# Layer 0 sum pass: TensorE works on pairs of half tiles, and SyncE and GpSimd share the stacking of the keys

## What is computed

```python
q = (query @ Wq + bq).reshape(B, Nq, H, D).transpose(0, 2, 1, 3)      # 16 heads of width 16
k = (key_value @ Wk + bk).reshape(B, Nkv, H, D).transpose(0, 2, 1, 3) # 12544 keys
v = (key_value @ Wv + bv).reshape(B, Nkv, H, D).transpose(0, 2, 1, 3)
attn = softmax(clip(einsum('bhqd,bhkd->bhqk', q, k) * scale, -CLAMP, CLAMP))
x = einsum('bhqk,bhkd->bqhd', attn, v).reshape(B, Nq, Cq) @ Wo + bo
```

## Time and profile before

| | us |
|---|---|
| median of 3 runs (lowest, highest) | 1162.57 (1161.85, 1162.88) |
| the profiled execution | 1163.62 |
| its span in the trace | 1161.8 |
| sum pass of layer 0 in it | 264.2 to 644.5 |
| one chunk of it, undisturbed | 26.6 |
| everything after it | 517.3 |

### The profile page before, as it was taken

The page is one execution under the profiler, slowest core; times in us unless marked ns, Lnnn a source line. Parts: engine busy times, 40 slices in busy tenths (PEclk is TensorE's granted clock), DMA queues, the critical chain, the costliest instruction groups (busy, mean ns, idle before and its releaser), DMA issues.

```text
span 1161.8 us, 21208 instructions
## 1 busy us (share of the span) xinstructions
PE 958.8 (83%) x7648; PEld 702.1 (60%) x7651; DVE 645.5 (56%) x936; ACT 539.8 (46%) x626; POOL 176.2 (15%) x93
## 2 busy tenths in 40 slices
PE   3877888749899999999969578886999979998514
PEld 2544555537677777777747365555777767776403
DVE  4777999862111222222250237994779757777592
ACT  2787888626666666666646313002333323332011
POOL 4000000141111111111193031242004030000000
PEclk9978999878999999999999689998999989999665
DMA  7213121154556555566614332211001000000000
GB/s 209 82 30 120 48 70 57 33 126 95 129 128 152 131 126 126 134 146 145 144 32 97 109 101 56 64 36 32 1 5 33 1 6 1 1 1 1 1 0 5
DMA packets 37319, 81.73 MB, mean 70 GB/s; under 512 B 9553, under 2 KB 17426, under 8 KB 37138
## 3 DMA queue, kind: packets, MB, share of 16 engines
q1 hardware_dynamic: 37266, 81.01, 28.1%
HBM read 41.54 MB, written 0.13 MB: 36 GB/s over the span
## 4 chain that ended last, share of the span: by engine, by line
PE 46%; issue 19%; DVE 11%; SPq 9%; DMA 7%; ACT 6%; POOL 1%; DVEq 1%; ACTq 0%; POOLq 0%
PE ps L1498 10%; SPq L310 8%; DMA ks<-khl 6%; PE ps L1508 6%; PE ps L1291 5%; PE ps L1519 5%; PE ps L1303 4%; PE ps L1273 4%; PE ps L1245 4%; PE ps L1500 2%; DVE cm L813 2%; ACT pr L555 1%; DVE pr L819 1%; DMA raw<-in_ctxT 1%; PE ps L1282 1%
## 5 line engine op out<-in xcount | busy, mean ns | idle before, releaser
L617 ACT ACTIVATE pr<-ps 128x1024 f32<-128x1024 f32 x196 | 200.0, 1026 | 131.7 <-DVEq L966 127.9
L1291 PE MATMUL ps<-qs,ks 128*128 128x256 f32 x784 | 147.0, 310 | 21.8 <-DMA ks<-khl 13.9
L1245 PE MATMUL ps<-ks 128*128 128x448 f32 x448 | 134.5, 422 | 33.7 <-ACT pr L555 14.3
L1291 PEld LDWEIGHTS ps<-qs,ks 128*128 128x128 f32 x784 | 106.8, 192 | 64.2 <-issue 33.0
L695 ACT ACTIVATE pr<-ps 128x1024 f32<-128x1024 f32 x56 | 57.5, 1027 | 184.7 <-DVE ps L1096 184.7
L1498 PE MATMUL ps<-ks,ct 128*128 128x512 f32 x448 | 128.3, 408 | 7.2 <-issue 4.6
L813 DVE TENSOR_REDUCE cm<-ps 128x1 f32<-128x896 f32 x112 | 120.5, 1084 | 16.9 <-PE ps L1245 16.0
L1245 PEld LDWEIGHTS ps<-ks 128*128 128x128 f32 x448 | 80.7, 206 | 76.8 <-DVE cm L813 28.0
L1303 PE MATMUL ps<-pr,v 128*17 128x128 f32 x3136 | 124.6, 277 | 0.2 <-ACT pr L617 0.2
L847 DVE SCALAR_TENSOR_TENSOR khl<-ps,bk,khl 128x448 fp32r<-128x448 f32 x56 | 38.2, 682 | 151.0 <-ACT khl L592 151.0
L1096 DVE TENSOR_SCALAR ps<-ps 128x1024 f32<-128x1024 f32 x56 | 68.9, 1231 | 76.5 <-PE ps L1500 76.5
(11 more groups left out here) (259 smaller groups left out, 1325.6 us busy)
## 6 DMA issues: line engine op xcount, KB each, us to landing
ks<-khl SPq DMA_DIRECT2D x168, 224.0 KB, 4.8
raw<-in_ctxT SPq DMA_DIRECT2D x36, 448.0 KB, 3.7
raw<-in_ctxT SPq DMA_DIRECT2D x54, 224.0 KB, 4.2
ffw<-in_mask_q SPq DMA_DIRECT2D x1, 1568.0 KB, 10.0
ffw<-in_W1T SPq DMA_DIRECT2D x1, 1024.0 KB, 4.9
ffw<-in_W2T SPq DMA_DIRECT2D x1, 1024.0 KB, 7.2
pr<-in_Wq SPq DMA_DIRECT2D x1, 1024.0 KB, 5.1
pr<-in_Wkt SPq DMA_DIRECT2D x1, 1024.0 KB, 7.4
```

The lines of the kernel that those rows point to most:

```text
L617: nc.scalar.activation(pr[:, (HALVES * b + u) % 4, :], bank(2 * (u % 2), 2), ACT.Exp).then_inc(S["e0_exp"], 1)
L1245: last = mm(ps[:, bank + n, 0:NB], qn[:, h, :], kn[:, b, t, n * NB:(n + 1) * NB], start=True, stop=True)
L1291: last = mm(ps[:, 2 * z + k // 2, (k % 2) * 256:(k % 2) * 256 + 256], ks_v[:, b, gg, t * P:(t + 1) * P], qs[:, gg * 256:gg * 256 + 256], s ...
```

## The change

TensorE now handles half tiles in pairs (`chunk0` and `projections0`): two scores, then up to two key blocks or two value tiles of the next chunk, then two weighings. The value tiles alternate between banks 7 and 5. The tables of key and value positions are per pair. SyncE issues only the eight high transfers, and waits for ScalarE's last high block (`e0_khi`) in place of VectorE's low one; GpSimd's own queue issues the four low transfers (`stack_low_keys`), behind a one-element addition, ahead of `split_lo0` of the chunk after. ScalarE's copy of the raw context comes in two parts, after half tiles 7 and 9, and GpSimd's remainder waits for the second as before.

```diff
-KEYS_AT = [0, 1, 2, 3]
-VALUES_AT = [4, 5, 6, 7, 8, 9, 10]
+KEYS_AT = [[0, 1], [2, 3], [], [], [], [], []]
+VALUES_AT = [[], [], [0, 1], [2, 3], [4, 5], [6], []]
...
             def stack_keys(c, b):
-                sp.wait_ge(S["e0_klo"], 4 * c + 6)
+                sp.wait_ge(S["e0_khi"], 4 * c + 4)
...
-                for slot, part in ((0, 0), (1, 0), (2, 1)):
+                for slot in range(2):
...
+            def stack_low_keys(c, b):
+                pool.wait_ge(S["e0_klo"], 4 * c + 6)
+                pool.wait_ge(S["e0_score"], HALVES * (c + 1))
+                nc.gpsimd.tensor_tensor(pause[:, 2:3], pause[:, 1:2], pause[:, 1:2], ALU.add
+                                        ).then_inc(S["e0_low_go"], 1)
+                for g in range(4):
+                    pool.dma_start(ks_v[64:96, b, g::4, :].bitcast(F32),
+                                   khl[32 * g:32 * g + 32, 1, :, :].bitcast(F32)
+                                   ).then_inc(S[f"e0_low_keys{b}"], 16)
+                pool.wait_ge(S["e0_low_go"], c + 1)
...
-                    if keys and u - 1 in KEYS_AT:
-                        i = KEYS_AT.index(u - 1)
-                        key_block_hi(c + 1, i, 22 + 11 * (c + 1) + K_ORDER[i], (f"e0_keys{b}", 192 * (i2 + 1)))
-                    if split and u == 9:
-                        split_hi0(c + 2, b)
+                    if keys and 2 <= u < 6:
+                        i = u - 2
+                        key_block_hi(c + 1, i, 22 + 11 * (c + 1) + K_ORDER[i], (b, i2 + 1))
+                    if split and u in (7, 9):
+                        split_hi0(c + 2, b, halves=[(u - 7) // 2])
...
-                    if nxt:
-                        if u - 1 in KEYS_AT:
-                            key_block_lo(c + 1, KEYS_AT.index(u - 1))
-                        if u in VALUES_AT:
-                            t = VALUES_AT.index(u)
+                    if nxt and u % 2 == 1 and u > 1:
+                        for i in KEYS_AT[(u - 3) // 2]:
+                            key_block_lo(c + 1, i)
+                        for t in VALUES_AT[(u - 3) // 2]:
                             value_tile(c + 1, 1 - b, t, 22 + 11 * (c + 1) + V_ORDER[t])
...
+            def chunk0(c, b, i2, nxt):
+                for v in range(TPC):
+                    if v < TPC - 1:
+                        scores0(c, b, 2 * v + 2)
+                        scores0(c, b, 2 * v + 3)
+                    elif nxt:
+                        pe.wait_ge(S["ks_ones"], 2)
+                        pe.wait_ge(S[f"e0_keys{1 - b}"], 128 * (i2 + 1 + b))
+                        pe.wait_ge(S[f"e0_low_keys{1 - b}"], 64 * (i2 + 1 + b))
+                        scores0(c + 1, 1 - b, 0)
+                        scores0(c + 1, 1 - b, 1)
+                    if nxt:
+                        projections0(c + 1, 1 - b, v)
+                    weigh0(c, b, 2 * v)
+                    weigh0(c, b, 2 * v + 1)
```

More of the change, by code:

```diff
@@ L64, with value_bank @@
 PAIRS = [(W_AH, X_AH), (W_AL, X_AH), (W_AH, X_AL), (W_BH, X_B), (W_BL, X_B)]
-KEYS_AT = [0, 1, 2, 3]
-VALUES_AT = [4, 5, 6, 7, 8, 9, 10]
-K_ORDER = [1 + sorted(KEYS_AT + VALUES_AT).index(u) for u in KEYS_AT]
-V_ORDER = [1 + sorted(KEYS_AT + VALUES_AT).index(u) for u in VALUES_AT]
+KEYS_AT = [[0, 1], [2, 3], [], [], [], [], []]
+VALUES_AT = [[], [], [0, 1], [2, 3], [4, 5], [6], []]
+K_ORDER = [1, 2, 3, 4]
+V_ORDER = [5, 6, 7, 8, 9, 10, 11]
+def value_bank(t):
+    return 7 if t % 2 == 0 else 5
 TURNS = ["x0", "o0", "x1", "x2", "x3", "x4", "o4", "x5"]
@@ L414, in _ @@
             pool.wait_ge(S["e0_lo"], 3)
+            stack_low_keys(0, 0)
             pool.wait_ge(S["m0_ml"], 1)
@@ L418, in _ @@
             pool.wait_ge(S["ks_ones"], 2)
-            with pool.Fori(2, NCH, 2) as c:
+            with pool.Fori(0, NCH - 2, 2) as c:
                 for b in range(2):
-                    split_lo0(c + b, b)
+                    stack_low_keys(c + b + 1, 1 - b)
+                    split_lo0(c + b + 2, b)
+            stack_low_keys(NCH - 1, 1)
             pool.wait_ge(S["thr"], 1)
@@ L531, in key_block_max0, with split_hi0 @@
                                      bias=bk0[:, t:t + 1]).then_inc(S["m0_keys"], 1)
[L533 to L537, removed]
+            def split_hi0(c, b, halves=(0, 1)):
+                if 0 in halves:
+                    act.wait_ge(S["e0_raw"], 48 * (c + 1))
+                    act.wait_ge(S["e0_proj"], 11 * c + 11)
+                    nc.scalar.copy(ct[:, b, X_AH, :], raw[:, 0, :])
+                if 1 in halves:
+                    nc.scalar.copy(ct[:, b, X_B, :], raw[:, 1, :]).then_inc(S["e0_hi"], 1)
             def mask_sum(s):
@@ L1318, in _ @@
                     t = h - 8
-                    values0(0, 0, t, bank=7 if t % 2 == 0 else 4, emptied=1 if t == 0 else 0)
+                    pe.wait_ge(S["e0_v"], t + (1 if t == 0 else 0))
+                    values0(0, 0, t, 7 if t % 2 == 0 else 4)
             pe.wait_ge(S["m0_ml"], 1)
@@ L1341, in _ @@
             pe.wait_ge(S["ks_ones"], 1)
-            pe.wait_ge(S["e0_keys0"], 192)
+            pe.wait_ge(S["e0_keys0"], 128)
+            pe.wait_ge(S["e0_low_keys0"], 64)
             scores0(0, 0, 0)
[L1347 to L1364, removed]
-                step0(c, b, HALVES - 1, True, False)
-                step0(c + 1, 1 - b, 0, nxt, False)
-                weigh0(c, b, HALVES - 1)
+            def projections0(c, b, v):
+                for i in KEYS_AT[v]:
+                    if i == 0:
+                        pe.wait_ge(S["e0_v"], TPC * c)
+                    project0(c, b, i)
+                for t in VALUES_AT[v]:
+                    if t == 1:
+                        pe.wait_ge(S["e0_klo"], 4 * c + 5)
+                    pe.wait_ge(S["e0_v"], TPC * c + t + (1 if t == 0 else 0))
+                    values0(c, b, t, value_bank(t))
@@ L1369, in _ @@
             pe.wait_ge(S["nm"], 2)
-            step0(0, 0, 0, True, False)
+            scores0(0, 0, 1)
             pe.wait_ge(S["zero"], 1)
@@ L1376, in _ @@
                 for b in range(2):
-                    round0(2 * i2 + b, b, i2, True)
-            round0(NCH - 2, 0, NSUP - 1, False)
-            for u in range(1, HALVES):
-                step0(NCH - 1, 1, u, False, True)
-            weigh0(NCH - 1, 1, HALVES - 1)
+                    chunk0(2 * i2 + b, b, i2, True)
+            chunk0(NCH - 2, 0, NSUP - 1, True)
+            chunk0(NCH - 1, 1, NSUP - 1, False)
             pe.wait_ge(S["o0_read"], 1)
```

11 lines of the change are left out of this document (6 added, 5 removed).

## The result

| | before | changed |
|---|---|---|
| median, us (20 runs each) | 1162.37 | 1165.67 |
| lowest to highest | 1159.51 to 1164.24 | 1161.76 to 1168.78 |
| the profiled execution, its span | 1163.62, 1161.8 | 1168.78, 1167.0 |

The ratio is 1.003, with a 95% interval of 1.002 to 1.004: slower by 3.3 us between the medians. The forecast was 1116, so this is the place of rival 1. The profiled execution is the slowest of the 20, so the sums over its trace show a somewhat larger loss.

A forecast was written before the change was run, and what follows sets the result against it. TensorE and the stacking of keys were both taken as nearly at the limit in layer 0's sum pass. Savings of 47 us from 1163.6 gave 1116.5, about 1116 against the median; forecast range 1106 to 1127, wide range 1106 to 1166.

The forecast's parts named there:

- rival 1: Queues share DMA engines, S stays 15.1, TensorE idles 3.0 us a chunk, clock falls: 1172 us (1160 to 1177); chance 0.20.
- the pairs on TensorE: Layer 0's sum pass: a pair saves 0.3 us of switching; rounds 4.2 and 3.3 us, TensorE needs 23.4 a chunk.
- the sum: Savings added: chunk 0 -3.0, chunks 1 to 11 at 23.7 us each -33.7, chunk 12 -9.4, chunk 13 -1.0; together -47.
- the first transfer: First stacking transfer issued 11.2 us after the chunk's start, against 11.3 before: nothing gained.
- Chunk 12: 29.5 us for 38.87: 23.7, plus 4.3 for VectorE's table, plus 1.5 for unpackings; gain 9.4, bounds 4 and 11.
- Chunk 13: Bare chunk, 19.2 us before: six pairs save at most 2 us, taken as 1.
- S: Time from first stacking transfer's issue to last one's landing: 15.1 us before, forecast up to 12.5, bounds 10.7 and 15.1.
- The copy in two parts: ScalarE's split copy of the raw context fits the pauses between exponentials and costs nothing.
- the raw load: Next raw context load on SyncE, behind GpSimd's remainder, has a chunk's time to spare.
- the clock: In rival 1: TensorE's clock falls to 0.50 behind each long pause, priced at 1.6 us a chunk.
- Chunk 0: First chunk of the sum pass: forecast 27.9 to 24.9 us, -3.0; rival 1 put it at +1.
- Sign (b): While both queues run, DMA exceeds 300 GB/s; the last high transfer lands under 12.5 us after the first issue.

## Why the prediction was wrong

**Right: the pairs on TensorE.** Rounds of 4.2 and 3.3 us were forecast, 4.18 and 3.33 measured; 23.4 us a chunk, and 23.54 measured once nothing else was late. The switch saved per pair was taken as 0.3, and 1.92 / 7 is 0.27. The 23.7 of the sum is a slip of 0.1 (the mean of 23.4 and 11.2 + 12.5 is 23.6), worth 1 us.

**Right: the first transfer,** at 11.2, at full clock (11.1 with the filled pause). "Nothing is gained here" held.

**Chunk 12: the number near, in part by luck.** It took 28.18 us for 29.5. Right is that GpSimd's ternary work has moved behind the chunk's keys, 18.5 us of it into chunk 13, and that VectorE's unpackings then take their shortest, 0.28 to 0.29. But the table, said to stay at +4.3, did not stay: it went from 6.1 us (585.19 to 591.25) to 3.5 (600.51 to 603.97), with GpSimd's work gone from beside it, and the first exponential came 2.2 us after the scores instead of 5.2. And it is not TensorE that sets the 28.2 us but the stack, 12.6 to its first transfer and 15.5 for itself. With the stack out of the way the chunk takes 27.53. Chunk 13 gave 0.3 where 1 was taken; it begins behind a pause of 3.3 us, at a clock of 0.91 over the chunk.

**Wrong: the stack.** S was taken at 12.5 or less, "nearer to the lower end, since the row at 358 is stacking itself". It is 15.3, or 15.5 with the start of the scores. The step that failed takes the full overlap from a row of half a microsecond at a seam between two transfers. The row is real, and the changed kernel has such stretches (312 GB/s), but they don't last. As far as the orders tried tell, they come while the two queues have transfers of different halves of the partitions. Over a stack that is worth 0.4 to 0.8 us (the queues alone, 14.3 to 14.7 for 15.1), 1.7 in their last ordinary chunk, not 4.4. The rows at 209 and 358, both at a share over 1, could not say which pairs of transfers overlap; the bound of 15.1 was the honest end, and the value should have stayed near it. The rule of the Trainium skill (DMA: Bandwidth & Descriptors, "Issuing engines are not separate DMA queues"), which the prediction weighed and put at 0.20, agrees with the result to within these 0.8 us. In the section "Rules for kernel authors" of the same page the Trainium skill says of two transfers to disjoint halves of the partitions that they serialize. Here that is nearly so, and goes a little too far: at one busy share the order moved the rate between 227 and 246 GB/s on one queue and between 215 and 258 on two.

**Wrong: "The copy in two parts fits the pauses between exponentials: nothing", and the raw load has "a chunk's time to spare".** Being early was a harm. ScalarE's second copy ended 22.0 us after the chunk's start before, and ends 19.0 after it now (426.37 + 0.94 - 408.28); GpSimd's remainders end 3 us earlier with it, and the raw load, which they release, falls into the stack. Only about 0.9 of the 3 us is the first half of the copy, which no longer stands in front of the second; the rest comes with the pairs. By these figures, as an estimate, the load would go out a microsecond later without the copy in two parts, and still inside the stack. Price: 0.7 to 0.9 us a stack, and 1150 instead of 1165.7 where it is taken out. It has eaten what the second queue brought.

**Left out of the forecast, priced in rival 1: the clock.** A chunk was put at 23.7 and took 27.85 (306.4 / 11). Of the 4.15 between them, 3.0 are the stack (15.5 for 12.5) and 1.2 are TensorE's slow rounds ahead of the first transfer (12.36 for 11.2). Rival 1 had S = 15.1, a pause of 3.0 us (measured 2.6 to 3.1), a clock of 0.50 behind it (0.59 over 3.3 us), chunks 1 to 11 at 308 (measured 306.4). It put the end at 1172 and, if half the lost time hides, at 1164. Chunk 0 was worse than it said, +3.9 for +1: the clock is 0.71 up to its first transfer, which goes at 278.64, 14.6 us after the start (before, 0.80 and 12.2), and its stack takes 16.9 us (15.6 before). Chunk 12 was better, -10.7 for -4. The mechanism and its price were there; what was wrong was the chance, since it hung on one number, S, whose decision point was 14.8. That the measured 1165.7 still lies in the wide range of 1106 to 1166 is no merit of the forecast: the way was the other one.

**Sign (b) decided it:** the last high transfer was to land in under 12.5 us, with over 300 GB/s while both queues run. It landed after 15.3, with 245 over six us.

## What to carry over

A wait that covers work is a dependency with an end time: making the engine beside it faster gives nothing until that end moves, and here it took something, since the longer idle piece lowered TensorE's clock. The pairs alone made the kernel 25 us slower, and they made it 24 us faster once the stack began 4 us earlier; so look for an earlier start (cut the transfer, send what is ready) before hoping for a faster transfer, and then check that the issuing engine keeps up. And bound an unknown transfer rate by its sustained row, not by its best half microsecond.

## What the hardware showed unexpectedly

- **The rate of a row of transfers depends on their order.** Twelve transfers confined to 32 partitions each, on one queue, move 227 GB/s in order of their slots and 246 alternating between the halves, over the same five us of a stack and at the same busy share of the engines; they land 1.1 and 0.98 us apart.
- **Filling a pause helps.** Ten matmuls that compute nothing take 13 us off the changed kernel.
- **Issuing costs differ.** SyncE takes 0.636 us per stacking transfer of 112 KB. GpSimd takes 0.53 (2.15 us for four of 224 KB), the unknown for which the prediction allowed 1 us and tried 4; it was harmless, the low transfers landing 4.4 us ahead of the last high one.
- **VectorE's small instructions are slower beside GpSimd's work.** The seven one-element additions of the table take 2.87 us at the start of chunk 12 before, where GpSimd is busy throughout, and 1.24 us in the changed kernel, where it stands idle; one unpacking instruction takes up to 2.42 us and 0.29.
